# Other slots for the weight quantization between the attention tiles of an eight-core transformer layer

## Chip, cores and metric

The kernel runs on the 8 cores of one Trainium2 chip. Each core works alone on 2048 of the 16384 rows of x. The metric is the device time in microseconds of the slowest core.

## The reference

```
x = layernorm(x + attn(x));  x = layernorm(x + ffn(x))        # x: (2, 8192, 1024)
attn: Q = (x @ Wq + bq) * scale;  K = (x @ Wk + bk) * scale;  V = x @ Wv + bv
      w = softmax(Qr @ Kr);  a = (w @ Vr).reshape(B, L, D);  return a @ Wo + bo
      # 16 heads of width 64, cut by plain reshapes of (B, L, D)
ffn:  Wq1 = quantize(W1) (4096x1024);  Wq2 = quantize(W2) (1024x4096)
      quantize(W) = clip(round(W / (mean(abs(W)) + 1e-5)), -1, 1)
      h = relu(x @ Wq1.T + b1);  return h @ Wq2.T + b2
```

The plain reshapes make every head a run of 512 rows of x: 512 rows times 1024 columns give 8192 positions of width 64. A core therefore handles four independent heads, which its code calls batches.

## The kernel before

Every engine has its own list of instructions, written out by a Python program in one order; each list is executed in order, and waits on semaphores tie the lists together. SP and GpSimd issue nearly all DMAs.

The four batches (b = 0 to 3) run one after another. A batch transposes its 512 rows of x, computes Q, K and V (folded by DMA into tensors 8192 wide) and transposes V. Then come 16 query tiles (qt = 0 to 15) of 512 queries. For one tile TensorE computes scores for 32 groups of 256 keys (L524, L529), ScalarE takes the exponential of each group (L537), and TensorE multiplies with V and sums into a PSUM bank (PV, L550 and L555), two groups behind the scores. The sum of the exponentials is row 64 of the same bank. Two banks of ps_pv alternate between tiles, so PV of tile q may start only when tile q-2 has been read out.

The readout of a tile is on VectorE: the reciprocal of the sums (L563), then GpSimd writes it to DRAM and loads it back spread over 64 partitions (L566, L572), then VectorE multiplies and writes A2 (L578), which frees the bank, and GpSimd copies A2 to the other 64 partitions (L583).

Behind that, VectorE gets steps of the weight quantization. There are 129, in a fixed list of which each call of emit_qstep() takes the next: 64 gamma steps, a finalize step, and 64 quantizing steps, 32 of W1 and then 32 of W2. A gamma step loads 512 KB of a weight into Wch on SP and adds up absolute values (L254, L256). The finalize step goes through DRAM four times on GpSimd to make the thresholds. A quantizing step loads 512 KB into Wch on SP and makes two halves of 512 columns: two comparisons (L342, L345) and a subtraction into qout (L348), then a DMA on SP writes qout to DRAM (L272 for W1, L275 for W2). There is one Wch and one qout: a load waits for the step before, and a half waits for the write of the half before. The next tile's reciprocal stands behind all this in VectorE's list.

After the 16 tiles of a batch come four tiles of the output projection (tc = 0 to 3; L622, L630, read out in halves by L639 and L644, after an x load on SP) and the layer norm. The first two tiles' norms are done there. Those of tiles 2 and 3 are deferred into the next batch: the sums and variance of the first at qt = 2, its scaling (L682) and the second's sums at qt = 4, the second's scaling at qt = 6, ahead of that tile's groups in each engine's list. ScalarE makes 1/sqrt of the variance in between. At qt = 6 GpSimd waits for both x1 writes and issues a bf16 copy of the batch's x1 in DRAM.

After batch 3 the quantized weights are loaded transposed and the two FFN matmuls run over four batches of 512 rows, with no quantization left.

Of the kernel before, what the change touches and what calls it, by code (L numbers as in the profile page):

```python
# [47 lines left out]
def build_nc():  # L48
# [106 lines left out]
    with ExitStack() as es:  # L155
# [204 lines left out]
        for b in range(NB):  # L360
# [132 lines left out]
            for qt in range(QTB):  # L493
# [90 lines left out]
                    A2[64:128, qt * 512:qt * 512 + 512],  # L584
                    A2[0:64, qt * 512:qt * 512 + 512]), sG, 16)
                wp[("a2dup", qtg)] = (sG, ad)
                emit_qstep()
                emit_qstep()
                if 8 <= qt < 12:
                    emit_qstep()  # L590
                    emit_qstep()

# [312 lines left out]
```

How the kernel before makes its waits and increments, by code:

```python
    def w(self, eng, sem, v):  # L27
        if v > 0:
            self.L[eng].append(lambda e, s=sem, vv=v: e.wait_ge(s, vv))
# [1 line left out]
    def add(self, eng, f, inc=None, n=1):  # L31
        if inc is None:
            self.L[eng].append(f)
            return None
        tot = self.c[id(inc)] = self.c.get(id(inc), 0) + n
        self.L[eng].append(lambda e, ff=f, s=inc, nn=n: ff(e).then_inc(s, nn))
        return tot
```

## Time and profile before

| | us |
|---|---|
| median of 3 runs (3281.42 to 3285.01) | 3281.52 |
| the profiled execution's own time | 3285.15 |
| span of its slowest core (core 5) | 3283.6 |
| spans of the eight cores | 3267.4 to 3283.6 |
| TensorE busy, share of span | 2756.8 (84%) |
| ScalarE busy | 1949.3 (59%) |
| VectorE busy | 914.6 (28%) |
| mean granted clock of the cores | 0.930 to 0.932 |

The span runs from the first to the last instruction of one core, the time also holds what lies around it. The busy shares are means over stages with different limits. A row of the timeline names the start and length of an instruction in microseconds and, in brackets, how long its engine was idle before it and what ended that. A reciprocal (L563) marks the end of each query tile, so the distance from one to the next is the time of a tile.

### The profile page before, as it was taken

What the parts mean: (1) busy time and instruction counts of PE and PEld (TensorE: products, weight loads), DVE (VectorE), ACT (ScalarE), POOL (GpSimd) and SP (SyncE); (2) the same over time, 40 slices, a digit from 0 to 9 for tenths busy, and PEclk for the clock granted to TensorE, in tenths of its full rate; (3) what the DMA queues carried; (4) which work ended last, traced back from release to release, by engine and by line L of the source; (5) the groups of instructions that cost most, each with busy time, mean ns of one, the idle gap of its engine ahead of it and who ended that gap; (6) DMA issues with size and microseconds to landing.
All of it is one profiled execution on the core that took longest, in us unless ns stands there. A gap on an engine that the chain in (4) does not pass through costs nothing.

```text
span 3283.6 us, 40735 instructions; the slowest of 8 cores (3267.4 to 3283.6 us)
## 1 busy us (share of the span) xinstructions
PE 2756.8 (84%) x12064; PEld 893.7 (27%) x12064; DVE 914.6 (28%) x1371; ACT 1949.3 (59%) x2307; POOL 153.3 (5%) x282
## 2 busy tenths in 40 slices
PE   0899999948999998577999877479999993999998
PEld 0322222213222222122222212132222221444443
DVE  0212223232132223321333333322311112443343
ACT  0089999910999998207999876019999990000000
POOL 3000000000000000000000000000000000000000
PEclk9899999968999999788999988689999996999999
DMA  8401112124012112250122222341210007811111
GB/s 114 73 19 44 47 48 81 47 61 71 25 44 66 53 53 82 80 71 23 55 80 66 75 78 67 65 71 36 62 39 8 8 6 144 147 45 58 39 39 45
DMA packets 171946, 191.59 MB, mean 58 GB/s; under 512 B 113248, under 2 KB 129632, under 8 KB 171616
## 3 DMA queue, kind: packets, MB, share of 16 engines
q1 hardware_dynamic: 141536, 158.37, 19.7%
q0 software_dynamic: 30208, 30.62, 5.4%
q8 instruction: 115, 1.88, 0.2%
q14 instruction: 87, 0.71, 0.1%
HBM read 125.93 MB, written 37.88 MB: 50 GB/s over the span
## 4 chain that ended last, share of the span: by engine, by line
ACT 41%; PE 24%; DMA 13%; issue 11%; DVE 7%; SPq 2%; ACTq 1%; POOL 1%; DVEq 0%; POOLq 0%
ACT PT L537 40%; PE ps_sb L791 7%; PE ps_pv L737 7%; PE ps_pv L435 4%; DMA x_bf<-x 2%; DMA Wch<-W 2%; DMA x_tc<-x 1%; DVE rec_sb L563 1%; PE ps_tr L476 1%; SPq L599 1%; DMA rec_bc<-recscr 1%; PE ps_sb L524 1%; PE ps_pv L550 1%; DMA wq<-qout 1%; ACTq L29 1%
## 5 line engine op out<-in xcount | busy, mean ns | idle before, releaser
L537 ACT ACTIVATE PT<-ps_sb 128x1024 bf16<-128x1024 f32 x2048 | 1891.0, 1104 | 135.3 <-PE ps_sb L529 133.2
L550 PE MATMUL ps_pv<-PT,VsT 128*65 128x512 bf16 x2048 | 832.7, 407 | 64.5 <-DVE A L578 43.6
L524 PE MATMUL ps_sb<-Qd,Kd 64*128 64x512 bf16 x2048 | 762.1, 377 | 77.9 <-ACT PT L537 70.2
L529 PE MATMUL ps_sb<-Qd,Kd 64*128 64x512 bf16 x2048 | 788.3, 390 | 0.0
L555 PE MATMUL ps_pv<-PT,VsT 128*65 128x512 bf16 x2048 | 782.6, 382 | 0.0
L524 PEld LDWEIGHTS ps_sb<-Qd,Kd 64*128 64x128 bf16 x2048 | 185.5, 93 | 934.0 <-issue 934.0
L563 DVE RECIPROCAL rec_sb<-ps_pv 1x512 f32<-1x512 f32 x64 | 214.5, 3352 | 695.9 <-PE ps_pv L555 693.3
L550 PEld LDWEIGHTS ps_pv<-PT,VsT 128*65 128x65 bf16 x2048 | 221.6, 108 | 561.2 <-issue 561.2
L737 PE MATMUL ps_pv<-x1T,WqT 128*128 128x512 bf16 x1024 | 230.5, 389 | 27.3 <-DMA x1T<-x1bfscr 14.4
L828 ACT ACTIVATE uln<-vareps 128x1 f32<-128x1 f32 x16 | 3.2, 203 | 412.3 <-DVE vareps L824 412.3
L555 PEld LDWEIGHTS ps_pv<-PT,VsT 128*65 128x65 bf16 x2048 | 228.6, 112 | 0.0
L791 PE MATMUL ps_sb<-WqT,hT 128*128 128x512 bf16 x1024 | 226.6, 379 | 0.0
L482 ACT COPY VsT<-ps_tr 128x64 bf16<-128x64 bf16 x128 | 27.2, 213 | 306.9 <-PE ps_tr L476 306.9
L529 PEld LDWEIGHTS ps_sb<-Qd,Kd 64*128 64x128 bf16 x2048 | 185.0, 93 | 0.0
L677 ACT ACTIVATE uln<-lnva 128x1 f32<-128x1 f32 x16 | 3.8, 235 | 299.0 <-DVE lnva L669 299.0
L622 PE MATMUL ps_sb<-bo_row,ones 1*128 1x512 bf16 x32 | 17.4, 544 | 159.2 <-DVE s L644 99.6
L342 DVE TENSOR_SCALAR tq<-Wch,thrbc 128x512 bf16<-128x512 f32 x128 | 61.8, 483 | 318.4 <-DMA Wch<-W 178.0
L578 DVE SCALAR_TENSOR_TENSOR A<-ps_pv,rec_bc 64x512 bf16<-64x512 f32 x64 | 43.7, 683 | 371.1 <-DMA rec_bc<-recscr 371.1
L737 PEld LDWEIGHTS ps_pv<-x1T,WqT 128*128 128x128 bf16 x1024 | 102.0, 100 | 155.3 <-issue 40.2
L748 DVE TENSOR_SCALAR hT<-ps_pv,b1c 128x512 bf16<-128x512 f32 x128 | 95.8, 751 | 142.7 <-PE ps_pv L737 142.7
L791 PEld LDWEIGHTS ps_sb<-WqT,hT 128*128 128x128 bf16 x1024 | 97.7, 98 | 120.5 <-issue 7.3
L391 PE MATMUL ps_tr<-eye,x_bf 128*128 128x128 bf16 x128 | 30.9, 256 | 117.7 <-DMA x_bf<-x 100.8
(90 smaller groups left out, 1237.1 us busy)
## 6 DMA issues: line engine op xcount, KB each, us to landing
Wch<-W SPq DMA_DIRECT2D x128, 512.0 KB, 4.1
Qd<-Qtm SPq DMA_DIRECT2D x32, 256.0 KB, 6.1
Kd<-Qtm SPq DMA_DIRECT2D x32, 256.0 KB, 6.2
rec_bc<-recscr POOLq DMA_DIRECT2D x64, 128.0 KB, 2.8
x_tc<-x SPq DMA_DIRECT2D x16, 512.0 KB, 5.1
wqt<-qout SPq DMA_DIRECT2D x64, 128.0 KB, 1.7
wq<-qout SPq DMA_DIRECT2D x64, 128.0 KB, 1.8
x1f<-x1scr SPq DMA_DIRECT2D x16, 512.0 KB, 4.0
```

The lines of the kernel that those rows point to most:

```text
L342: sch.add(v, lambda e, cp=cp, hh=hh: e.tensor_scalar(tq1[:, :], Wch[:, hh * 512:hh * 512 + 512], thrbc[:, cp:cp + 1], None, ALU.is_gt), sVE)
L435: tm = sch.add(t, lambda e, W_sb=W_sb, fc=fc, tc=tc, dh=dh, n=n: e.matmul(ps_pv[n % 2][:, :], xT[:, fc * 512 + tc * 128:fc * 512 + tc * 12 ...
L524: sch.add(t, lambda e, cc=cc, qt=qt, hh=hh: e.matmul(ps_sb[:, hh:hh + 512], Kd[0:64, cc * 128:cc * 128 + 128], Qd[0:64, qt * 512:qt * 512 ...
L529: ts = sch.add(t, lambda e, cc=cc, qt=qt, hh=hh: e.matmul(ps_sb[:, hh + 512:hh + 1024], Kd[64:128, (cc + 1) * 128:(cc + 1) * 128 + 128], Q ...
L537: ex = sch.add(sc, lambda e, gg=gg: e.activation(PT[:, (gg % 4) * 1024:(gg % 4) * 1024 + 1024], ps_sb[:, (gg % 2) * 1024:(gg % 2) * 1024 + ...
L550: sch.add(t, lambda e, pg=pg, qtg=qtg: e.matmul(ps_pv[qtg % 2][0:65, :], VsT[:, (2 * pg) * 65:(2 * pg) * 65 + 65], PT[:, (pg % 4) * 1024:( ...
L555: sch.add(t, lambda e, pg=pg, qtg=qtg: e.matmul(ps_pv[qtg % 2][0:65, :], VsT[:, (2 * pg + 1) * 65:(2 * pg + 1) * 65 + 65], PT[:, (pg % 4) ...
L563: rc = sch.add(v, lambda e, qtg=qtg: e.reciprocal(rec_sb[0:1, :], ps_pv[qtg % 2][64:65, :]), sREC)
L578: vn = sch.add(v, lambda e, qtg=qtg, qt=qt: e.scalar_tensor_tensor(A2[0:64, qt * 512:qt * 512 + 512], ps_pv[qtg % 2][0:64, :], 1.0, rec_bc ...
L737: tm = sch.add(t, lambda e, oc=oc, dc=dc: e.matmul(ps_pv[oc % 2][:, :], WqT1[:, dc * 4096 + oc * 128:dc * 4096 + oc * 128 + 128], x1T[:, d ...
L748: ev = sch.add(v, lambda e, oc=oc: e.tensor_scalar(hT[:, oc * 512:oc * 512 + 512], ps_pv[oc % 2][:, :], b1c[:, oc:oc + 1], 0.0, ALU.add, A ...
L791: tm = sch.add(t, lambda e, tsub=tsub, dh=dh, oc=oc: e.matmul(ps_sb[:, (tsub % 2) * 1024 + dh * 512:(tsub % 2) * 1024 + dh * 512 + 512], h ...
```

## The change

It moves calls of emit_qstep(). Before, each query tile has two, and tiles 8 to 11 have four. After, tiles 2 to 11 have four each and the other six none. The list of steps, and what a step does, are as before.

```
-                emit_qstep()
-                emit_qstep()
-                if 8 <= qt < 12:
+                if 2 <= qt < 12:
+                    emit_qstep()
+                    emit_qstep()
                     emit_qstep()
                     emit_qstep()
```

## Rows read from the trace of the kernel before

**Rows 1.** The profile's page: its span and busy time of each engine.
```profile
span 3283.6 us, 40735 instructions; the slowest of 8 cores (3267.4 to 3283.6 us)
...
PE 2756.8 (84%) x12064; PEld 893.7 (27%) x12064; DVE 914.6 (28%) x1371; ACT 1949.3 (59%) x2307; POOL 153.3 (5%) x282
```

**Rows 2.** Busy time by window: length, PE, PEld, DVE, ACT, POOL, clock, DMA, GB/s.
```profile
1538.00:2042.00 504.00, 444.94 (x1922) 125.36 (x1920) 167.47 (x273) 444.06 (x484) 23.68 (x46) 0.96 0.24 69
...
2245.00:2706.00 461.00, 438.57 (x1921) 125.23 (x1920) 91.96 (x98) 442.88 (x484) 23.68 (x46) 1.00 0.10 28
```

**Rows 3.** VectorE's timeline, batch 1: start us, us, instruction, [idle before <-releaser].
```profile
1102.03 3.35 DVE L563 RECIPROCAL rec_sb<-ps_pv 1x512 f32<-1x512 f32 x1 [13.89 <-PE ps_pv L555]
...
1132.68 3.35 DVE L563 RECIPROCAL rec_sb<-ps_pv 1x512 f32<-1x512 f32 x1 [1.98 <-PE ps_pv L555]
...
1163.51 3.35 DVE L563 RECIPROCAL rec_sb<-ps_pv 1x512 f32<-1x512 f32 x1 [1.82 <-PE ps_pv L555]
...
1220.22 3.35 DVE L563 RECIPROCAL rec_sb<-ps_pv 1x512 f32<-1x512 f32 x1 [0.24 <-DVE qout L348]
...
1262.69 3.35 DVE L563 RECIPROCAL rec_sb<-ps_pv 1x512 f32<-1x512 f32 x1 [0.24 <-DVE qout L348]
...
1334.11 3.35 DVE L563 RECIPROCAL rec_sb<-ps_pv 1x512 f32<-1x512 f32 x1 [0.24 <-DVE qout L348]
```

**Rows 4.** VectorE's timeline, batch 2, reciprocals of tiles 2, 8, 9, 11, 12, 15.
```profile
1600.07 3.35 DVE L563 RECIPROCAL rec_sb<-ps_pv 1x512 f32<-1x512 f32 x1 [2.81 <-PE ps_pv L555]
...
1784.46 3.35 DVE L563 RECIPROCAL rec_sb<-ps_pv 1x512 f32<-1x512 f32 x1 [7.17 <-PE ps_pv L555]
...
1830.87 3.35 DVE L563 RECIPROCAL rec_sb<-ps_pv 1x512 f32<-1x512 f32 x1 [0.24 <-DVE qout L348]
...
1920.62 3.35 DVE L563 RECIPROCAL rec_sb<-ps_pv 1x512 f32<-1x512 f32 x1 [0.24 <-DVE qout L348]
...
1965.14 3.35 DVE L563 RECIPROCAL rec_sb<-ps_pv 1x512 f32<-1x512 f32 x1 [0.24 <-DVE qout L348]
...
2041.53 3.35 DVE L563 RECIPROCAL rec_sb<-ps_pv 1x512 f32<-1x512 f32 x1 [0.24 <-DVE qout L348]
```

**Rows 5.** TensorE's timeline, batch 2, around the first PV of tiles 13, 14, 15.
```profile
1930.38 0.61 PE L550 MATMUL ps_pv<-PT,VsT 128*65 128x512 bf16 x1 [12.34 <-DVE A L578]
...
1931.88 0.64 PE L550 MATMUL ps_pv<-PT,VsT 128*65 128x512 bf16 x1
...
1975.23 0.61 PE L550 MATMUL ps_pv<-PT,VsT 128*65 128x512 bf16 x1 [12.03 <-DVE A L578]
...
2005.22 0.38 PE L555 MATMUL ps_pv<-PT,VsT 128*65 128x512 bf16 x1
...
2007.57 0.41 PE L550 MATMUL ps_pv<-PT,VsT 128*65 128x512 bf16 x1
```

**Rows 6.** VectorE's timeline, batch 2, deferred normalization ahead of tile 4's reciprocal.
```profile
1654.66 0.76 DVE L682 TENSOR_SCALAR x<-s,rstd 128x1024 f32<-128x1024 f32 x1 [0.18 <-DVE qout L348]
...
1659.11 0.15 DVE L669 TENSOR_SCALAR lnva<-varsum 128x1 f32<-128x1 f32 x1
```

**Rows 7.** DMA issues: tensors, queue, kind, count, KB each, median us to landing.
```profile
x1bfscr<-x1scr POOLq DMA_DIRECT2D x4, 1024.0 KB, 9.3
```

**Rows 8.** VectorE's timeline, ends of batches 0, 1, 2.
```profile
664.24 3.35 DVE L563 RECIPROCAL rec_sb<-ps_pv 1x512 f32<-1x512 f32 x1 [13.83 <-PE ps_pv L555]
...
684.51 0.69 DVE L639 SCALAR_TENSOR_TENSOR s<-ps_sb,x_tc 128x512 f32<-128x512 f32 x1 [0.24 <-DVE s L644]
...
1363.42 0.69 DVE L639 SCALAR_TENSOR_TENSOR s<-ps_sb,x_tc 128x512 f32<-128x512 f32 x1 [0.24 <-DVE s L644]
...
2073.03 0.69 DVE L639 SCALAR_TENSOR_TENSOR s<-ps_sb,x_tc 128x512 f32<-128x512 f32 x1 [0.24 <-DVE s L644]
```

**Rows 9.** TensorE's timeline, second half of the projection's first tile, batch 2.
```profile
2058.60 1.95 PE L630 MATMUL ps_sb<-Wo_sb,A 64*128 64x512 bf16 x16
```

**Rows 10.** Busy time by window, one stalled tile of batch 2; columns as above.
```profile
1930.00:1975.00 45.00, 31.22 (x128) 8.44 (x128) 14.55 (x27) 29.87 (x32) 1.54 (x3) 0.84 0.26 75
```

## The prediction, made before the changed kernel was run

> **What bounds the kernel now.** I read the page first, then busy time over windows cut from the first to the last reciprocal of a batch's 16 query tiles, then the timeline of VectorE tile by tile, and last TensorE's and GpSimd's around the stalls. The page gives the span and three engines' shares: TensorE 84%, ScalarE 59%, VectorE 28% [rows 1]. No engine is full, so the bound differs by stage. In batch 3 the 15 tile intervals take 461 us, 30.7 us a tile, with the clock at 1.00 [rows 2], and in batch 0 the same; that is the pace of the loop of scores, exp and PV. In batch 2 the same work takes 504 us at a clock of 0.96, and in batch 1 478 us (1102.03 to 1334.11 is 232 us for seven tiles, where seven free tiles take 215) [rows 2, 3].
>
> The reader is to see why in VectorE's rows. After a four-gamma tile VectorE waits 1.98 and 1.82 us for the next PV, at 1132.68 and 1163.51, so four gamma steps just fit into a tile [rows 3]. The tile with the finalize step and three quantizing steps takes 56.7 us (1163.51 to 1220.22), one with four W1 quantizing steps 42.47 us (1220.22 to 1262.69); the idle time before these next reciprocals is 0.24 us, so VectorE and the DMA round trips inside its queue set the pace [rows 3]. In batch 2 a tile with four steps takes 46.41 us for the first and, for the next three, (1965.14 - 1830.87) / 3 = 44.76 us [rows 4]. VectorE is hardly computing there: a step waits for its 512 KB load, then between its halves for the write of qout. TensorE pays: PV of a tile q may start only when A2 of tile q-2 is written. It stood idle 12.34 and 12.03 us for that [rows 5].
>
> **What the change moves.** Each batch has 40 slots before (16x2 + 4x2) and after (10x4), so each batch runs the same steps: batch 0 gamma 0 to 39; batch 1 gamma 40 to 63, finalize, 15 quant steps; batch 2 40 quant steps (17 of W1, 23 of W2); batch 3 the last nine. Nothing is removed. Slots leave tiles 0, 1 and 12 to 15, and tiles 2 to 7 get four where they had two. Every step brings its load and two output DMAs on SP and its work on VectorE; GpSimd's queue is touched only by finalize. What stands behind a step is the next tile's reciprocal on VectorE, then its two GpSimd round trips, A2, and PV two tiles on.
>
> The slack: PV of tile q+2 would start 2 x 30.7 + 2.0 - 30.7 = 32.7 us after the undisturbed reciprocal of q (the 2.0 is the gap from one tile's last PV, 2005.60, to the next one's first, 2007.57) and needs 9.8 to 10.1 us from that reciprocal to A2 (1920.62 to 1930.38, 1965.14 to 1975.23) [rows 4, 5]. So VectorE may be some 22 us late for nothing. Four W1 steps are 42.5 - 30.7 = 11.8 us over a tile, four W2 steps 14: two such tiles in a row eat the slack, and from then on each costs its overrun in full.
>
> When the loaded tiles end (tile 11), the rest is no longer VectorE's: from the reciprocal of tile 12, PV of 14 starts 10.1 us on, takes 30.4 (1975.23 to 2005.60), PV of 15 another 30.7, and 0.2 to its reciprocal: 71.4 us. Batch 1 before shows exactly this, 1334.11 - 1262.69 = 71.42 [rows 3, 5].
>
> *Batch 0.* Four gammas fit a tile, nothing is lost: 0.
>
> *Batch 1.* Gamma in tiles 2 to 7 fits too (28.9 of 30.7 us). The normalization deferred from the batch before adds 4.85 us ahead of tile 4's reciprocal (1654.66 to 1659.26 plus 0.24) [rows 6], late by under 3 us and won back at 2 us a tile. Finalize moves from tile 10 to tile 8, quantizing fills 9, 10, 11. Reciprocal 12 comes at 1102.03 + 56.7 + 3 x 42.47 = 1286.1 instead of 1262.69: +23.5, and the 71.4 that follow are the same.
>
> *Batch 2.* From reciprocal 2 at 1600.07: tiles 2 to 5 with 16 W1 steps, 4 x 42.47 = 169.9; tile 6 as the mixed tile, 46.4; tiles 7 to 11, 5 x 44.76 = 223.8. The normalization was hidden in idle time and now lies on the path: 4.85 us at tile 4 and 0.8 at tile 6. GpSimd waits at tile 6 for the x1 write (issued after that 0.76 us row) before it issues the bf16 copy, and the scratch write of tile 6's reciprocal is behind it. Before, the reciprocal came later than all this; now it follows at once. Nothing shows the price, between 0 and the copy's median landing of 9.3 us [rows 7]; I take 4, nearer the low end, because GpSimd waits only for the x1 write and issues the copy without waiting for it. Sum 1600.07 + 449.8 = 2049.9, plus 71.4 gives 2121.3 for reciprocal 15 against 2041.53: +79.8. ScalarE, in order, will stand at the head of tile 6 for the variance of the second deferred tile, which VectorE computes ahead of reciprocal 4: from reciprocal 3, the head of tile 6 is reached at 9.8 + 30.6 = 40.4 us, the variance is there at 42.5 + 4.8 = 47.3, about 7 us later; but PV of 6 waits for A2 of 4 until 57, so this costs 0.
>
> *Batch 3.* Two full tiles (2 and 3, W2 steps), one step in tile 4. With t for reciprocal 2: reciprocal 4 at t + 2 x 44.76 + 4.85 = 94.4, PV of 6 at 104.2 instead of 3 x 30.7 + 2.0 = 94.1: 10 us, and 1.9 more because a tile's PV after a stall takes 30.6 us instead of 28.7: +12. The next tiles are free again.
>
> *The end of each batch.* Before, tile 15's two steps stand on VectorE and SP ahead of the output projection, whose x load is behind them on SP. From reciprocal 15 to the second evacuation of the projection it was 684.51 - 664.24 = 20.3, 29.3 and 31.5 us in batches 0, 1, 2 [rows 8]. Without steps only TensorE holds it: in batch 2 it had both halves done at 2058.60 + 1.95 = 2060.55, 19.0 us after the reciprocal [rows 4, 9]. Gain 1.3, 10.3, 12.5: 24 us. Batch 3 had no step there: 0.
>
> Sum: 23.5 + 79.8 + 12 - 24 = +91 us. The profiled execution took 3285.15 us (span 3283.6), 3.6 over the median of the runs, 3281.52; by its own time 3376, by the median 3373.
>
> The granted clock enters here. A stalled tile starts at half clock (PV to PV 1.50 us, 1930.38 to 1931.88), and the mean of such a tile is 0.84 [rows 5, 10]. That is 1.2 GHz for the first microseconds after 12 us idle and 2.4 GHz for the rest, and the 1.9 us a tile hide inside a 44 us interval of VectorE.
> The Trainium skill (TensorE: Matmul & The Clock Gate, "HAM oscillation — how this bites in real kernels") has a rule against this change: matmul bursts parted by waits can run throttled every time. By that rule alone the whole tile would be slow, the half-clock rival below; the rows show the clock coming back within the tile, so I weigh it low.
>
> **The rivals.**
> *The half clock holds.* If TensorE stayed at 1.2 GHz through stalled tiles, 32 groups of 1.50 us make 48 us and the pace would be TensorE's: 10 tiles of batch 2 at 50 instead of 44, three of batch 1 at 50 instead of 42.5, the two closing tiles in each 19 us longer: +60 + 22 + 76, about 3530 at worst, 3450 if only the loaded tiles. For it: idle 12 us in each of ten tiles. Against: mean clock 0.84 in such a tile [rows 10]. Chance 0.03.
> *The lateness is absorbed.* It ends on the faster side. If four steps fit beside A2 in a tile (under 30.7 - 9.7 = 21 us), nothing stalls and the 24 us at the ends stay: 3258. Gamma does fit; a W1 quartet takes 33 us, W2 35. It decides at 30.7 us a tile. Chance 0.02.
> *Stall is only moved.* The steps a batch are the same, so the stalls could stay the same sum: 3281 to 3285. This needs VectorE to be busy without a break in tiles 0 to 7 before; it was idle before reciprocals there (2.81 us at 1600.07, 7.17 at 1784.46), and the 20 us of tiles 0, 1 and 12 to 15 are now unused [rows 4]. Chance 0.02.
> *Less of it.* All quartets at the W1 price (-14), batch 3 inside the slack (-12), the copy free (-4): down to 3343. Chance 0.09.
> *More of it.* The early tiles share DMA with the x1 writes and the copy, quartets at 46.4 (+8 on five tiles, +16 on four), the copy 9 us: up to 3405 and over. Chance 0.09.
> *My forecast*, 0.75.
>
> **How the numbers follow.** 3373 is the likeliest case. The range 3348 to 3400 takes in the price of a quartet from 42.5 to 46.4 us, the copy, batch 3 and most of the two nearest rivals. Differences under 0.2% (6.6 us) can't be told from no change. Faster 0.02, same 0.02, slower 0.96.
>
> **What would show it.** Reciprocal to reciprocal in batch 2: 42 to 45 us in each of ten intervals from tile 2 on, TensorE idle about 12 us before PV for A2 in tiles 5 to 13; tiles 13 to 15 free; reciprocal 15 near 583 us after reciprocal 0 (503 before). Batch 1: stall from tile 8 on, 255 us from reciprocal 8 to 15 (232). Batch 3: one stall of about 10 us at tile 6. First projection evacuations 17 to 19 us after reciprocal 15 in all four batches. It is wrong if a quartet is cheaper when it repeats, if the clock doesn't recover, or if another queue (SP with the x1 writes) sets the pace.

## The result, and the profile after

The changed kernel is slower: the ratio of its runs to those of the kernel before is 1.031 (95% interval 1.0298 to 1.0322), the medians are 3386.85 and 3284.63 us. In some executions one die or both ran at a lower clock; ratios and profiles leave those out, the medians don't. The profiled execution took 3386.8 us, 101.7 more than the one before. The forecast was 91 more, 3373 in a range of 3348 to 3400.

The page of the changed kernel:

```profile
span 3385.3 us, 40674 instructions; the slowest of 8 cores (3372.2 to 3385.3 us)
...
PE 2768.6 (82%) x12003; PEld 894.0 (26%) x12064; DVE 916.2 (27%) x1371; ACT 1952.5 (58%) x2307; POOL 153.3 (5%) x282
...
L550 PE MATMUL ps_pv<-PT,VsT 128*65 128x512 bf16 x2048 | 839.3, 410 | 175.8 <-DVE A L578 154.9
```

The same group of instructions in the kernel before:

```profile
L550 PE MATMUL ps_pv<-PT,VsT 128*65 128x512 bf16 x2048 | 832.7, 407 | 64.5 <-DVE A L578 43.6
```

The engines are busy for nearly as long as before [rows 1]: no work was added. TensorE now stands 154.9 us before PV until A2 is written, 43.6 before. Busy time by window, one window a batch, from the first to the last reciprocal (columns as in rows 2):

```profile
202.10:663.00 460.90, 438.33 (x1920) 125.17 (x1916) 114.76 (x110) 442.31 (x480) 23.18 (x45) 1.00 0.17 53
857.70:1360.80 503.10, 445.55 (x1920) 125.15 (x1916) 141.11 (x189) 444.51 (x484) 26.44 (x51) 0.96 0.21 59
1555.10:2144.60 589.50, 454.20 (x1920) 125.40 (x1916) 172.60 (x285) 446.10 (x484) 23.68 (x46) 0.89 0.22 63
2335.80:2807.50 471.70, 439.82 (x1920) 125.10 (x1916) 92.02 (x98) 443.26 (x484) 23.67 (x46) 0.99 0.10 28
```

Batch 2 takes 589.5 us against 502.9 (the 504.00 of [rows 2] is the width of a rounded window) and batch 3 471.7 against 461 [rows 2], batch 1 503.1 against 478 (1334.11 less its first reciprocal at 856.03). Between the batches the last reciprocal to the next first one takes 194.7, 194.4 and 191.2 us (before 191.8, 204.5, 203.8). The first row has the times before, the others the changes. The third is the slowest core of each profiled execution, core 5 before and core 6 after; the last is the mean of all eight cores after less that of all eight before:

| us | batch 0 | end 0 | batch 1 | end 1 | batch 2 | end 2 | batch 3 | sum |
|---|---|---|---|---|---|---|---|---|
| before | 461.0 | 191.8 | 478.1 | 204.5 | 502.9 | 203.8 | 460.9 | |
| forecast change | 0 | -1.3 | +23.5 | -10.3 | +79.8 | -12.5 | +12 | +91 |
| measured change, slowest core | 0 | +2.9 | +25.0 | -10.1 | +86.5 | -12.6 | +10.9 | +103 |
| measured change, mean of cores | 0 | +1.3 | +23.3 | -9.5 | +86.8 | -11.7 | +13.2 | +103 |

The two rows agree on the sum and, within 3 us, on each term; differences of 1 to 3 us between single terms are differences between cores. In the row of the slowest core, what is left, -1.2 us ahead of batch 0's last reciprocal and +0.4 behind batch 3's, gives the 101.7 by and large. In the following, intervals are those of the slowest core. VectorE's timeline of batch 2, the reciprocals and one row of the deferred normalization (columns as in rows 3):

```profile
1616.59 3.35 DVE L563 RECIPROCAL rec_sb<-ps_pv 1x512 f32<-1x512 f32 x1 [17.38 <-PE ps_pv L555]
...
1659.92 3.35 DVE L563 RECIPROCAL rec_sb<-ps_pv 1x512 f32<-1x512 f32 x1 [0.24 <-PE ps_pv L555]
...
1703.73 0.75 DVE L682 TENSOR_SCALAR x<-s,rstd 128x1024 f32<-128x1024 f32 x1 [0.18 <-DVE qout L348]
...
1708.36 3.35 DVE L563 RECIPROCAL rec_sb<-ps_pv 1x512 f32<-1x512 f32 x1
...
1750.96 3.35 DVE L563 RECIPROCAL rec_sb<-ps_pv 1x512 f32<-1x512 f32 x1 [0.24 <-DVE qout L348]
...
1795.04 3.35 DVE L563 RECIPROCAL rec_sb<-ps_pv 1x512 f32<-1x512 f32 x1
...
1847.42 3.35 DVE L563 RECIPROCAL rec_sb<-ps_pv 1x512 f32<-1x512 f32 x1 [0.24 <-DVE qout L348]
...
1894.28 3.35 DVE L563 RECIPROCAL rec_sb<-ps_pv 1x512 f32<-1x512 f32 x1 [0.24 <-DVE qout L348]
...
2073.23 3.35 DVE L563 RECIPROCAL rec_sb<-ps_pv 1x512 f32<-1x512 f32 x1 [0.24 <-DVE qout L348]
...
2082.91 3.35 DVE L563 RECIPROCAL rec_sb<-ps_pv 1x512 f32<-1x512 f32 x1
...
2144.59 3.35 DVE L563 RECIPROCAL rec_sb<-ps_pv 1x512 f32<-1x512 f32 x1 [21.24 <-PE ps_pv L555]
```

From tile 2 on the intervals are 43.3, 48.4, 42.6, 44.1, 52.4 and 46.9 us, and the four from 1894.28 to 2073.23 have a mean of 44.7, as the three of [rows 4]; idle time before each is 0.24 us or none. From tile 12 the last three take 71.36 us. Before, 2 us of idle time or more stood ahead of the reciprocals of tiles 2 and 8 [rows 4].

Two intervals between reciprocals stand out. In the 48.4 the normalization's rows lie on the path (1703.73 to the reciprocal at 1708.36, 4.6 us and the gap before). The 52.4, tile 6, are explained by GpSimd's timeline:

```profile
1798.79 0.51 POOL L507 DMA_DIRECT2D x1bfscr<-x1scr  x1 [37.19 <-DVE rec_sb L563]
1799.29 0.49 POOL L566 DMA_DIRECT2D recscr<-rec_sb  x1
1809.62 0.53 POOL L572 DMA_DIRECT2D rec_bc<-recscr  x1 [9.84 <-DMA recscr<-rec_sb]
```

The 2 KB scratch write goes out right behind the 1 MB copy, and GpSimd waits 9.84 us for it; in an undisturbed tile of the next section it is 1.68. A2 of tile 6 comes 17.6 us after its reciprocal instead of 9.0. In this trace the copy landed 10.1 us after its issue, and the write, issued 0.5 us behind it, 0.17 us after the copy. The cores of all runs' traces hold 164 such pairs in which the write was issued at least 2.5 us before the copy landed: it went out 0.5 to 8.6 us behind the copy and landed 0.15 to 0.28 us after it each time. The small write comes in when the big one is through, whenever it was issued.
The Trainium skill (DMA: Bandwidth & Descriptors, "Two DMAs through the same engine are not ordered") says that within one queue of one DMA engine descriptors start in order. The trace agrees with it: the write's first packet starts at 1807.64 us, and the last of the copy's 32 had started at 1806.09.

TensorE's first PV behind a stall, tile 11 of batch 2, begins at half clock as in [rows 5]:

```profile
1948.26 0.61 PE L550 MATMUL ps_pv<-PT,VsT 128*65 128x512 bf16 x1 [12.42 <-DVE A L578]
...
1949.77 0.64 PE L550 MATMUL ps_pv<-PT,VsT 128*65 128x512 bf16 x1
```

And the end of batch 2, where the projection's read-out no longer waits for steps. It takes 19.9 us from the reciprocal to its second half (31.5 before [rows 4, 8]):

```profile
2161.39 0.69 DVE L639 SCALAR_TENSOR_TENSOR s<-ps_sb,x_tc 128x512 f32<-128x512 f32 x1 [6.89 <-PE ps_sb L630]
...
2164.51 0.69 DVE L639 SCALAR_TENSOR_TENSOR s<-ps_sb,x_tc 128x512 f32<-128x512 f32 x1 [1.64 <-PE ps_sb L630]
```

### The profile page after: what moved, and what is told of

Its sections match the earlier page's. It is cut to its first block, busy times and chain, and to the rows that moved or that the text cites. A ratio compares the mean times of both kernels' runs of the same rounds, so it can differ in the third digit from the quotient of the medians.

```text
span 3385.3 us, 40674 instructions; the slowest of 8 cores (3372.2 to 3385.3 us)
## 1 busy us (share of the span) xinstructions
PE 2768.6 (82%) x12003; PEld 894.0 (26%) x12064; DVE 916.2 (27%) x1371; ACT 1952.5 (58%) x2307; POOL 153.3 (5%) x282
## 4 chain that ended last, share of the span: by engine, by line
ACT 32%; PE 24%; DMA 19%; DVE 11%; issue 10%; SPq 2%; POOL 1%; ACTq 1%; DVEq 0%; POOLq 0%
ACT PT L537 31%; PE ps_sb L791 7%; PE ps_pv L737 6%; DMA Wch<-W 6%; PE ps_pv L435 4%; DMA x_bf<-x 2%; DVE rec_sb L563 2%; DMA wq<-qout 2%; DMA rec_bc<-recscr 2%; DVE tq L342 2%; DMA recscr<-rec_sb 2%; DMA wqt<-qout 2%; DVE qout L348 2%; DVE tq L345 1%; PE ps_tr L476 1%
## 5 line engine op out<-in xcount | busy, mean ns | idle before, releaser
L550 PE MATMUL ps_pv<-PT,VsT 128*65 128x512 bf16 x2048 | 839.3, 410 | 175.8 <-DVE A L578 154.9
L254 DVE TENSOR_REDUCE gtmp<-Wch 128x1 f32<-128x1024 f32 x64 | 77.8, 1215 | 193.9 <-DMA Wch<-W 193.9
```

Source lines behind the costliest of these rows:

```text
L254: ops.append((v, "sync", lambda e: e.reduce_sum(gtmp[:, :], Wch[:, :], AX.X, apply_absolute_value=True), sVE))
L550: sch.add(t, lambda e, pg=pg, qtg=qtg: e.matmul(ps_pv[qtg % 2][0:65, :], VsT[:, (2 * pg) * 65:(2 * pg) * 65 + 65], PT[:, (pg % 4) * 1024:( ...
```

## The experiments

My theory: a tile has 30.7 us; VectorE's queue, which holds its own work and the DMA round trips inside the steps, may be some 22 us late before PV waits; beyond that each tile over 30.7 us costs its overrun. Four quantizing steps behind one tile are called a quartet, a W1 or a W2 quartet by the weight. The rival theories: VectorE or the DMA engines are full; only the mean number of steps a tile counts; lateness is handed from batch to batch; the early tiles are crowded by other transfers.

**The copy out of the way.** At tile 6 the block that waits for the x1 writes and issues the copy is taken out and put in at tile 13:

```
+                if b > 0 and qt == 13:
+                    bb = b - 1
+                    sch.w(g, sX1W[0], wp[("x1w", bb, 2)][1])
+                    sch.w(g, sX1W[1], wp[("x1w", bb, 3)][1])
+                    sch.add(g, ...copy x1scr to x1bfscr..., sCB[bb], 16)
```

> Changed kernel, with GpSimd's bf16 copy of x1 moved from tile 6 to tile 13 of batches 1 to 3. Theory (the readout of tile 6 waits on GpSimd behind the x1 write and the copy, and with VectorE always late this lies on the path): A2 of tile 6 comes 9 us after its reciprocal instead of 16.7 and 17.6, reciprocal 8 of batch 1 comes 3 to 5 us earlier, batch 2 gets 8.7 us shorter; together 12 to 14 us under the changed kernel, about 3373. Rival (the scratch write is slow because the early tiles crowd the DMA rings, not because of the queue): A2 of tile 6 stays at 14 us or more, the time within 4 us of the changed kernel.

Measured: ratio to the kernel before 1.0265 (1.021 to 1.0321; 1.031 for the changed kernel), profiled execution 3369.1 us. GpSimd in tile 6 of batch 2:

```profile
1794.37 0.50 POOL L567 DMA_DIRECT2D recscr<-rec_sb  x1 [37.76 <-DVE rec_sb L564]
1796.55 0.53 POOL L573 DMA_DIRECT2D rec_bc<-recscr  x1 [1.68 <-DMA recscr<-rec_sb]
```

Batch 2 takes 577.1 us (-12.3, of which 8.3 in tile 6, whose interval is 44.1 instead of 52.4 us) and batch 1 501.5 (-1.6). Reciprocal 8 of batch 1 comes 2.9 us earlier, a little under the 3 to 5 expected, and 1.3 of it is lost again in the tiles behind the copy's new place. Over the means of the eight cores batches 1, 2 and 3 are 2.0, 8.8 and 2.2 us shorter and the span of a core 16.7, where 12 to 14 were expected; the rest of batch 2's 12.3 is the difference between one core and another. The wait comes from the copy, not from crowded early tiles: those kept their steps. Whether it is the order in GpSimd's queue or the copy's load on the DMA engines no run separates, since none puts the copy on another queue; that the write always lands 0.15 to 0.28 us after the copy speaks for the order. Tiles 12 and 13 have free time, so the copy's place there costs little (A2 of tile 13 of batch 2 comes 12.4 us after its reciprocal).

**The change in batch 2 alone.** A function gives the number of steps behind each tile, here and in the runs below:

```
+def slots(b, qt):
+    if b == 2:
+        return 4 if 2 <= qt < 12 else 0
+    return 4 if 8 <= qt < 12 else 2
...
+                for _ in range(slots(b, qt)):
+                    emit_qstep()
```

> The change in batch 2 alone; batches 0, 1 and 3 keep the slots of the kernel before. Theory (each batch pays for itself, W2 quartets back to back): reciprocal 0 to 15 of batch 2 takes 589 us against 503, its projection starts 12 us sooner, so 72 to 76 us over the kernel before, about 3358. Rival (part of batch 2's cost is handed on from batch 1): under 60 us over.

Measured: ratio 1.0211 (1.0165 to 1.0258), median 3353.96, 73.5 us over the kernel before on the same chip (3280.42). Batch 2 takes 587.2 us, the other three 461.0, 477.4 and 460.9, as before within 1 us. Each batch pays for itself, and the rival with under 60 us falls.

**Two qout tiles.** Changed slots; half hh writes qouts[hh] and waits for the write of its own tile:

```
+    qoutb = alloc("qoutb", [128, 512], BF16)
+    qouts = (qout, qoutb)
...
-                    if qstate["last_q_dma"] is not None:
-                        sch.w(v, *qstate["last_q_dma"])
+                    if qstate["last_q_dma"][hh] is not None:
+                        sch.w(v, *qstate["last_q_dma"][hh])
```

> Changed kernel, with two qout tiles, one for each half, so that no half waits for the write of the half just before. Theory (a tile's surplus is waiting inside VectorE's queue): a step gets about 1.95 us shorter, a W2 quartet takes 37 us instead of 44.8, a W1 quartet 34.7 instead of 42.4; the 22 us of slack swallow part: batch 2 about 510 to 520 us from reciprocal 0 to 15 instead of 589, batch 1 about 484 instead of 503, batch 3 461; 115 us under the changed kernel, about 3270 (3262 to 3285). Rival (VectorE or the DMA engines are full): the writes bunch up and the quartets stay over 42 us.

Measured: ratio 0.9965 (0.9931 to 1.0), profiled execution 3263.6 us. By the two ratios that is 3.45% of the time before, some 113 us, under the changed kernel, where 115 were expected. Two rows of a step of W2, the halves now close together, and the next load's wait:

```profile
1797.33 0.49 DVE L344 TENSOR_SCALAR tq<-Wch,thrbc 128x512 bf16<-128x512 f32 x1 [0.18 <-DVE qout L350]
...
1803.41 0.49 DVE L344 TENSOR_SCALAR tq<-Wch,thrbc 128x512 bf16<-128x512 f32 x1 [4.66 <-DMA Wch<-W]
```

The second half starts 0.18 us behind the first and waits for no write; the load's wait, 4.66 us here, is still there. W2 quartets take 35.7 to 36.9 us, W1 quartets 34.7 to 35.4. Batch 2 takes 505.4 us, batch 1 471.1, batch 3 460.9. The quartets are as expected; I had put batch 1 at 484 and batch 2 at 510 or more, too much by 13 and 5. Of the 13, 9.5 are the finalize tile, which got shorter too (47.8 us, 57.4 in the changed kernel); the 5 are not explained.

**Two load tiles as well.** The load of the next step is issued before the present one computes:

```
+        def wbuf(k):
+            return Wch[:, 0:1024] if k % 2 == 0 else x_tc[:, 1024:2048]
...
-                ld = sch.add(s, st[1], sS, 16)
-                sch.w(v, sS, ld)
+                issue_load(i)          # waits for the step before last, same tile
+                if not last:
+                    issue_load(i + 1)
+                k, ld = loaded[i]
+                sch.w(v, sLd[k % 2], ld)
```

> As the last, and with two load tiles as well, the second one in the half of x_tc that attention doesn't use; the load of the next step is issued before the present step computes. Theory: a step is 3 to 4 us, a quartet 21 to 26 us beside its readout, under 30.7; no stall in any batch, 461 us each: about 3200 (3190 to 3215). Rival (loads at this density share bandwidth among the cores of the chip and take longer): quartets of 30 us or more, batch 2 over 470 us.

Measured: ratio 0.9753 (0.9701 to 0.9805), median 3204.56. Batch 2 by window:

```profile
1508.20:1969.30 461.10, 438.38 (x1920) 125.27 (x1916) 172.58 (x284) 443.01 (x484) 23.68 (x46) 1.00 0.31 79
```

VectorE is busy for 172.58 us, as in the changed kernel's 589.5 us, and the DMA engines 0.31 of the time instead of 0.22: neither was full. The batches took 460.9 to 461.2 us on this core; on two others batch 1 took 464.6 and 462.3. So the slots of the change cost next to nothing once its steps don't wait.

**The same with the slots of before.** Only slots(b, qt) differs from the last run, 4 in tiles 8 to 11 and else 2, and with it which step is the last of a batch and issues no load ahead.

> The kernel before with its own slots, and two load tiles and two qout tiles. Theory (the slots matter only through waits inside a step): no stall either, 461 us a batch; only the two short steps of tile 15 stand ahead of the projection in three batches, 2 to 4 us each: within 10 us of the same edit on the changed slots, 3200 to 3212. Rival (the slots of the change cost something of their own): over 15 us apart.

Measured: ratio 0.98 (0.9783 to 0.9817), median 3214.29, a little over the 3212 expected; all batches 461. The ends of batches 1 and 2 are 198.1 and 196.7 us against 194.2 and 193.7, and on the mean of eight cores 4.2 and 5.7 us longer. The median is 9.7 us over the run with the change's slots, but that one ran on another chip and the intervals of the two ratios overlap. By the ends alone the change's slots would be a little better without the waits; the times don't show it.

**No tile overrun.** One load tile and one qout tile as in the kernel before:

```
+def slots(b, qt):
+    if b == 0:
+        return 4 if qt < 14 else 0
+    if b == 1:
+        return 4 if qt < 2 else 1 if qt == 2 else 2 if qt < 14 else 0
+    if b == 2:
+        return 2 if qt < 14 else 0
+    return 2
```

> Slots that overrun no tile, one load tile and one qout tile as before: four gamma steps in tiles 0 to 13 of batch 0 and 0, 1 of batch 1, finalize in tile 2, then two quantizing steps a tile, none in tiles 14 and 15 of batches 0 to 2. Theory (the cost is the overrun of a tile, and of tile 15): 461 us in all four batches and short ends; 3284.6 less 17 and 42 in batches 1 and 2, less 10 and 12 at their ends: 3198 to 3208. Rival (the deferred normalization, the copy or finalize stall it anyway): 3215 or more.

Measured: ratio 0.9766 (0.9749 to 0.9783), median 3202.71; taken again for a later comparison, 0.9759 (0.9744 to 0.9773), 3205.12. Batch 2 by window:

```profile
1511.70:1972.70 461.00, 438.25 (x1920) 125.15 (x1916) 140.87 (x213) 442.99 (x484) 23.68 (x46) 1.00 0.20 60
```

Slots alone, with no new buffer, take 2.3% off the kernel before. The normalization, the copy and finalize stall nothing here.

**Quartets in every second tile.** Gamma and finalize as in the last:

```
+    if b == 1:
+        return (4, 4, 1, 0)[qt] if qt < 4 else 4 if qt % 2 == 0 and qt < 13 else 0
+    return 4 if qt % 2 == 0 and qt < 13 else 0
```

> Gamma and finalize as in the last; then quartets of quantizing steps in every second tile, none between. Theory (VectorE may be 22 us late): a quartet is 12 to 14 us late and the free tile wins it back, no stall: 3198 to 3208, at most 4 more where the copy hits the quartet of tile 6. Rival (any tile over 30.7 us costs its overrun): 16 quartets x 13 us, over 3400.

Measured: ratio 0.9762 (0.9745 to 0.9778), median 3201.48, all batches 461. VectorE in tiles 0 to 2 of batch 2:

```profile
1509.40 3.35 DVE L571 RECIPROCAL rec_sb<-ps_pv 1x512 f32<-1x512 f32 x1 [33.24 <-PE ps_pv L563]
...
1551.48 3.35 DVE L571 RECIPROCAL rec_sb<-ps_pv 1x512 f32<-1x512 f32 x1 [0.24 <-DVE qout L356]
...
1570.86 3.35 DVE L571 RECIPROCAL rec_sb<-ps_pv 1x512 f32<-1x512 f32 x1 [5.97 <-PE ps_pv L563]
```

A quartet of 42.1 us and 19.4 us for the free tile are two tiles of 30.7. The interval behind tile 6 of batch 3 is 50.5 us, so the next reciprocal is 19.8 late, and still nothing is lost: the slack is at least that, and a tile may overrun.

**Quartets in pairs.** The same number of steps, 4, 4, 0, 0:

```
-        return (4, 4, 1, 0)[qt] if qt < 4 else 4 if qt % 2 == 0 and qt < 13 else 0
-    return 4 if qt % 2 == 0 and qt < 13 else 0
+        return (4, 4, 1, 0)[qt] if qt < 4 else 4 if qt % 4 < 2 and qt < 14 else 0
+    return 4 if qt % 4 < 2 and qt < 14 else 0
```

> Gamma and finalize as before; then quartets in two neighbouring tiles, two tiles free (4, 4, 0, 0). Theory: two quartets make 23 to 28 us of lateness, over the slack by 2 to 6, plus 1.9 for the slow start of PV, and more where the normalization (4.85) and the copy (8.7) fall in a pair: batch 1 469 to 478 us, batch 2 486 to 495, batch 3 468 or so; 40 to 58 us over the alternate one, 3240 to 3262. Rival (only the mean number of steps a tile matters): as the alternate one, 3200.

Measured: the fastest execution took 3266.16 and the profiled one 3274.57 us, 65 and 73 over the alternate kernel's median, where 40 to 58 were expected; no ratio with an interval could be formed. VectorE on its core 3, reciprocals of tiles 0 to 4 of batch 2:

```profile
1524.34 3.35 DVE L571 RECIPROCAL rec_sb<-ps_pv 1x512 f32<-1x512 f32 x1 [33.23 <-PE ps_pv L563]
...
1566.84 3.35 DVE L571 RECIPROCAL rec_sb<-ps_pv 1x512 f32<-1x512 f32 x1 [0.24 <-DVE qout L356]
1612.54 3.35 DVE L571 RECIPROCAL rec_sb<-ps_pv 1x512 f32<-1x512 f32 x1
1622.14 3.35 DVE L571 RECIPROCAL rec_sb<-ps_pv 1x512 f32<-1x512 f32 x1
1653.03 3.35 DVE L571 RECIPROCAL rec_sb<-ps_pv 1x512 f32<-1x512 f32 x1 [16.79 <-PE ps_pv L563]
```

TensorE's timeline there, the first PV of the tile that had to wait:

```profile
1622.26 0.61 PE L558 MATMUL ps_pv<-PT,VsT 128*65 128x512 bf16 x1 [3.77 <-DVE A L586]
```

Four tiles take 128.7 us instead of 122.9: two quartets are 88.2 - 61.4 = 26.8 late, TensorE waits 3.77 us for A2 and starts slowly, 5.8 in all. That gives the slack itself, 26.8 - 3.8 = 23.0 us, and 2.0 us for the slow start. Where the normalization and the copy join a pair it is more; batches 1 to 3 take 474.4, 499.8 and 473.4 us. The mechanism holds and the rival of the mean falls. My sum was right for batch 1 and 5 us too low for batches 2 and 3 each, so the time came out above its range.

**Steps left before the projection.** The kernel with no overrun, with two steps in tiles 14 and 15 of batches 1 and 2; beside it, on the same chip, that kernel again:

```
-        return 4 if qt < 2 else 1 if qt == 2 else 2 if qt < 14 else 0
-    if b == 2:
-        return 2 if qt < 14 else 0
+        return 4 if qt < 2 else 1 if qt == 2 else 2
```

> As the run with slots that overrun no tile (its median was 3202.7), but tiles 14 and 15 of batches 1 and 2 keep two quantizing steps each, so that two stand before the projection. Theory (steps of tile 15 delay the projection by 9 to 12 us in a batch with quantizing steps): the batches stay at 461 us from reciprocal 0 to 15, the second evacuation of the projection comes 29 to 31 us after reciprocal 15 instead of 19 to 20, and the time is 17 to 24 us longer, 3220 to 3227. Rival (the wait is made up later in the batch change, whose x loads are chained): under 8 us longer.

> The kernel of the run with slots that overrun no tile, beside the last one on the same chip. Theory: 3198 to 3208, and 17 to 24 us under the kernel with end steps. Rival: under 8 us apart.

Measured: ratios 0.9823 (0.9806 to 0.9839) and 0.9759 (0.9744 to 0.9773), profiled executions 3226.6 and 3205.6: 21.0 us. Ends 1 and 2 are 204.4 and 204.2 us against 194.0 and 190.1. The end of batch 2:

```profile
1981.43 3.35 DVE L571 RECIPROCAL rec_sb<-ps_pv 1x512 f32<-1x512 f32 x1 [5.99 <-PE ps_pv L563]
...
2012.38 0.69 DVE L644 SCALAR_TENSOR_TENSOR s<-ps_sb,x_tc 128x512 f32<-128x512 f32 x1 [4.60 <-DMA x_tc<-x]
...
2014.11 0.69 DVE L644 SCALAR_TENSOR_TENSOR s<-ps_sb,x_tc 128x512 f32<-128x512 f32 x1 [0.24 <-DVE s L649]
```

32.7 us to the second read-out, behind an x load that stood in SP's list behind the steps. This, 10 to 12 us in each of batches 1 and 2, is all the change gained.

## Why the prediction was right, point by point

- **The bound and the slack.** Right, and shown: two buffers for each wait take the stalls away with VectorE's busy time unchanged; quartets alternate for nothing, and in pairs cost 5.8 us for 26.8 of lateness. The slack, some 22 us by the prediction, is 23.0 by the pair, and 19.8 cost nothing. TensorE stood idle 7.5 to 20.8 us before the first PV of each of tiles 5 to 13 of batch 2, 12.5 on average, 12 forecast.
- **Batch 1**, +23.5 forecast, +25.0 measured. Four-gamma tiles fit. Reciprocal 8 came 248.9 us after reciprocal 0 instead of 246.0, since the copy delayed tile 6's readout (a 37.1 us interval) and only 3.4 of its 6.4 us were won back in the next tile; from there to 15 it took 254.1 us, 255 forecast.
- **Batch 2**, +79.8 forecast, +86.5 measured. Mis-sized terms: the copy, put at 4 us and measured at 8.6 (17.6 less 9.0), because I took it that a copy which GpSimd doesn't wait for holds little up, though I had named the write behind it, and that write lands only after the copy, so the upper end of my 0 to 9.3 us was the right one; and the W1 quartets, put at 42.47 and measured at 43.3, 43.6 (48.4 less 4.85), 42.6 and 44.1 less the 0.8, together 3 us more. In the other direction, tile 6 without the copy was 2.6 us under its 46.4; the W2 quartets of tiles 7 to 11 were together 2.0 over. The normalization and the 71.4 us of the end were right.
- **Batch 3**, +12 forecast, +10.9 measured (+13.2 on the mean of cores), one stall at tile 6, of 7.8 us where about 10 were forecast.
- **The ends.** Ends 1 and 2 -10.3 and -12.5 forecast, -10.1 and -12.6 measured, and shown by themselves in the last pair of runs. End 0 should have won 1.3 and lost 2.9, though its second read-out came 20.0 us after the reciprocal (20.3 before). The other cores show why: end 0 takes 190.7 to 194.4 us on the eight cores before and 191.4 to 194.7 after, and the slowest core was one of the short ones before and one of the long ones after. This is not put to the change.
- **The half clock.** Right that it recovers: batch 2's mean is 0.89 against 0.96. Its share of a stall, put at 1.9 us, comes to 1.7 by the prediction's own rows (PV in 30.4 us instead of 28.7), and was 2.0 where a run shows it by itself, in the pairs. In batch 2 it lay behind VectorE, whose quartets set the pace. The rival in which the clock holds at half falls.
The Trainium skill (TensorE: Matmul & The Clock Gate, "HAM oscillation — how this bites in real kernels") tells of short matmul bursts, parted by waits for DMA, that start throttled every time. The trace agrees that each burst behind a stall starts so (1.51 us from PV to PV). That by this rule a whole tile would be slow, as the prediction has it, goes beyond the page; no tile here was slow throughout.
- **Stall is only moved**, the rival at 0.02, is refuted: with the same steps in each batch as before, batches 1 to 3 lost 25, 86 and 11 us. Of *more of it*, the copy at 9 us nearly came true (8.6); quartets at 46.4 us did not, but for tile 7's 46.9 (the others 42.6 to 45.2, leaving out the tiles with the normalization and the copy).

## What to carry to other kernels

Side work in a consumer's queue has a price by the tile, not by the sum: take the period of the loop, the slack that the double buffer gives, and the time of the side work with its DMA round trips, and keep each run of tiles inside them. Spread it evenly or alternate it, and keep it away from the last tile before a stage that needs the same queues; here slots alone gave 2.3%, and two buffers for each wait gave about as much with either slots (2.5 and 2.0%). Don't put a large copy ahead of a small transfer that something waits for on the same queue.

## What the hardware showed beyond that

A 2 KB write issued by GpSimd 0.5 us behind its own 1 MB casting copy took 9.84 us until it was seen, 1.68 without the copy. In 164 pairs it landed 0.15 to 0.28 us after the copy, whether issued 0.5 or 8.6 us behind it. And TensorE, after 12.4 us of idle time, ran at 1.2 GHz (1.51 us from PV to PV) and came back to 2.4 GHz inside the same tile; nine stalls in a row, tiles 5 to 13 of batch 2, didn't make it stay low, with a granted clock of 0.89 over the batch.
